# A Mamba kernel whose end-of-chunk states are kept by DMA transfers from ScalarE's queue, where a ScalarE copy kept them

## The reference, cut to what matters

```
xc, z = split(x @ in_w.T);  xc = silu(causal_conv4(xc))
dt, B, C = split(xc @ xp_w.T);  dt = softplus(dt @ dtp_w.T + dtp_b)
h_t = exp(dt_t * A) * h_(t-1) + (dt_t * xc_t) * B_t     # 512 channels x 16 states
y_t = sum over the 16 states of h_t * C_t;  y = (y + xc * D) * silu(z);  out = y @ out_w.T
```

## Time and profile before

| | |
|---|---|
| median of 3 runs | 2550.9 us (2548.64 to 2559.86) |
| the profiled execution | 2551.9 us, span 2550.1 us |
| busy, share of the span | PE 85%, PEld 51%, DVE 74%, ACT 71%, POOL 63% |
| DMA queue that SP issues on | 129732 packets, 181.69 MB, 26.6% of 16 engines |
| `h_carry` copies on ACT | 256, median 193 ns |

### The profile page before, as it was taken

One profiled execution on the slowest core, in us unless ns is written; L12 is line 12 of the kernel. 1 busy time (PEld: TensorE's weight loads), 2 busy tenths in 40 slices (PEclk: granted clock), 3 DMA queues, 4 the chain that ended last, 5 costly groups with the idle time before them and its releaser, 6 DMA issues. The chain is left out here.

```text
span 2550.1 us, 40275 instructions
## 1 busy us (share of the span) xinstructions
PE 2180.0 (85%) x14544; PEld 1305.5 (51%) x14544; DVE 1894.2 (74%) x2586; ACT 1819.4 (71%) x3103; POOL 1615.2 (63%) x1407
## 2 busy tenths in 40 slices
PE   0798898988989989899898998987367699999967
PEld 0345454554545545455454554544234377887744
DVE  4389888898888988889888898888474455555543
ACT  0598889988899888998989989897162244444452
POOL 1089898898988989889898898989310411222010
PEclk9999999999999999999999999999668799999979
DMA  5404224043241532414314143140400211111031
GB/s 188 104 14 117 74 52 117 27 107 77 49 117 35 136 81 53 117 41 93 91 35 117 43 92 92 34 108 17 169 19 29 96 30 34 29 29 29 22 114 66
DMA packets 129930, 184.25 MB, mean 72 GB/s; under 512 B 13634, under 2 KB 76098, under 8 KB 129348
## 3 DMA queue, kind: packets, MB, share of 16 engines
q1 hardware_dynamic: 129732, 181.69, 26.6%
HBM read 134.97 MB, written 42.47 MB: 70 GB/s over the span
## 5 line engine op out<-in xcount | busy, mean ns | idle before, releaser
L617 POOL TENSOR_TENSOR h<-h,C_rep 128x512 f32<-128x512 f32 x1024 | 1274.3, 1277 | 199.4 <-ACT h_carry L536 199.4
L423 DVE TENSOR_TENSOR_SCAN h<-decay,h_carry,psum 128x512 f32<-128x512 f32 x768 | 956.1, 1271 | 126.2 <-PE psum L745 95.3
L528 ACT ACTIVATE decay<-dt_rep,A 128x512 f32<-128x512 f32 x1024 | 729.4, 713 | 101.0 <-DVE h L423 91.8
L745 PEld LDWEIGHTS psum<-ident,u_B 128*128 128x128 f32 x4096 | 476.7, 141 | 561.1 <-DVE h L423 310.2
L745 PE MATMUL psum<-ident,u_B 128*128 128x128 f32 x4096 | 630.4, 280 | 141.2 <-DVE h L423 109.0
L548 ACT ACTIVATE u_B<-u_tok,B_tok 128x512 f32<-128x512 f32 x832 | 589.2, 710 | 63.7 <-PE psum L745 45.9
L423 DVE TENSOR_TENSOR_SCAN h<-decay,zero,psum 128x512 f32<-128x512 f32 x256 | 319.0, 1271 | 54.3 <-PE psum L745 34.6
L754 PE MATMUL psum<-h,state_sum 128*32 128x512 f32 x2048 | 279.7, 619 | 11.1 <-POOL h L617 10.9
L606 POOL TENSOR_TENSOR u_B<-u_tok,B_tok 128x512 f32<-128x512 f32 x192 | 200.1, 1042 | 40.6 <-DVE u_tok L395 40.6
L1590 ACT ACTIVATE a_probs_T<-a_psum 128x512 f32<-128x512 f32 x128 | 76.4, 597 | 197.2 <-PE a_psum L1674 197.2
L1532 DVE TENSOR_REDUCE a_row_max<-a_psum 128x4 f32<-128x512 f32 x128 | 88.4, 691 | 143.3 <-PE a_psum L1665 143.3
(11 more groups left out here) (203 smaller groups left out, 2834.3 us busy)
## 6 DMA issues: line engine op xcount, KB each, us to landing
dt_rep<-dt_rows SPq DMA_DIRECT2D x256, 256.0 KB, 5.6
C_rep<-C_rows SPq DMA_DIRECT2D x256, 64.0 KB, 2.0
dt_rows<-x_dt_gated SPq DMA_DIRECT2D x16, 1024.0 KB, 4.8
x_tok<-mamba_residual SPq DMA_DIRECT2D x16, 512.0 KB
residual<-mamba_residual SPq DMA_DIRECT2D x16, 512.0 KB, 3.9
mamba_residual<-residual SPq DMA_DIRECT2D x16, 512.0 KB, 2.9
f_gru_weights<-in_slot_gru_dram SPq DMA_DIRECT2D x2, 2176.0 KB
n_x<-in_x_dram SPq DMA_DIRECT2D x4, 1024.0 KB, 10.8
```

What stands on the lines that cost most here:

```text
L423: dve.tensor_tensor_scan(h[:, slot(u)], dec[:, u % DEC], PS[:, u % 2], first, ALU.mult, ALU.add)\
L528: act.activation(dec[:, u % DEC], dtr[:, k % EG], ACT.Exp, scale=A[:, s // STEPS, k:k + 1]).then_inc(S["decay"], 1)
L617: pool.tensor_tensor(h[:, slot(u)], h[:, slot(u)], crep[:, k // EG], ALU.mult).then_inc(S["hc"], 1)
L745: ins = pe.transpose(PS[:, u % 2, tb * P:(tb + 1) * P], pr[:, f % 2, tb, eg], ident[:])
```

## The change

The copy in `keep` becomes a DMA that ACT issues, with the same source and destination. It is left out for the last chunk of a sequence (4 of the 16 steps), so 192 transfers take the place of 256 copies. Completion is signalled on four semaphores `h_carry_kept0` to `3` in turn, each raised by 16 by a transfer. POOL waits for the transfer of its quad, or in a last chunk for the four scans themselves. DVE waits for the transfer of the same quad of the chunk before.

```diff
+LANES = 4
+        kept = [sem(f"h_carry_kept{n}") for n in range(LANES)]
+        def last_chunk(q):
+            return q // QUADS % CHUNKS == CHUNKS - 1
+        def carries(q):
+            s = q // QUADS
+            return (s // CHUNKS * (CHUNKS - 1) + s % CHUNKS) * QUADS + q % QUADS
+        def carried(eng, q):
+            eng.wait_ge(kept[carries(q) % LANES], 16 * (carries(q) // LANES + 1))
...
                         if s % CHUNKS:
-                            at(dve, "carry", u // QT - QUADS + 1)
+                            carried(dve, u // QT - QUADS)
...
                 def keep(q):
-                    if not 0 <= q < ALL * QUADS:
+                    if not 0 <= q < ALL * QUADS or last_chunk(q):
                         return
                     at(act, "scan", QT * (q + 1))
                     k = QT * (q % QUADS)
-                    act.activation(carry[:, k:k + QT], h[:, slot(QT * q):slot(QT * q) + QT, T - 1], ACT.Copy)\
-                        .then_inc(S["carry"], 1)
+                    act.dma_start(carry[:, k:k + QT], h[:, slot(QT * q):slot(QT * q) + QT, T - 1], allow_slow_non_contiguous=True)\
+                        .then_inc(kept[carries(q) % LANES], 16)
...
                     if k % QT == 0:
-                        at(pool, "carry", u // QT + 1)
+                        if last_chunk(u // QT):
+                            at(pool, "scan", u + QT)
+                        else:
+                            carried(pool, u // QT)
```

More of the change, by code:

```diff
@@ L246, in mamba @@
                  "x_ev conv_mm conv halo xp_mm dbl silu z_mm z_ev sz dt_mm dt_raw dt bt_mm bt xcT_mm xcT dtT_mm uT skip_mm decay "
-                 "b scan carry hc ysum prod_a prod_p gated o_mm res").split()
+                 "b scan hc ysum prod_a prod_p gated o_mm res").split()
         S = {n: sem(n) for n in names}
         c_ld = [sem(f"C_loaded{n}") for n in range(NG)]
+        kept = [sem(f"h_carry_kept{n}") for n in range(LANES)]
         dtr_ld = [sem(f"dt_rep_loaded{ct}") for ct in range(CT)]
```

## The result

The changed kernel takes 2614.3 us (median of 4 runs, 2607.1 to 2622.8) against 2551.5 us: ratio 1.0242, 95% interval 1.0203 to 1.0281. It is slower, inside the forecast range and 17 us above the forecast number. The time came about as forecast in sign and size, but not where I had put it.

What follows compares the result with a forecast made beforehand. Each step was taken as three stretches in a row, bound by PE, then ACT, then DVE (with POOL). (2.1 + 0.5 + 1.5) x 12 = 49, less 3, on 2551.9 gave 2598 profiled, 2597 us median; range 2553 to 2645.

Steps and rivals of the forecast that it cites:

- ACT's side: ACT's queue: copies removed in its unbroken stretch gain 3 us in all; 192 transfer issues taken to cost nothing, at most 16.
- Term (a): Quad 9, kept at unit 44: POOL begins 2.2 us later for the landing, 2.1 us a step reaching the end.
- the 0.12 us of room: At quad 9: POOL's products ended at 824.98 and `states` began 0.12 us later, so that much lateness is hidden.
- Term (b): Quad 10, kept at 828.69 with the DMA engines busy: landing put at 3.5 us, costing 0.5 us a step.
- Term (c): Keeps while `dt_rep` fills the DMA engines, 842 to 856 us: late landings cost 1.5 us a step, between 0 and 4.0.
- the 3.1 of room: Keep at 843.11, while `dt_rep` comes in: 3.1 us of landing hidden by POOL's later start, `states`' 0.40 and PE's gaps.
- The last chunks: In 4 steps POOL no longer waits for ACT and starts quad 9 sooner: at most 5 us won, taken as nothing.
- B: Rival: no queueing, only the quad 9 landing costs: 2562 to 2573 us, to 2582 with quad 10; chance 0.22.
- C: Rival: full queueing of landings, or a slow issue on ACT besides: 2620 to 2653 us; chance 0.16.
- D: Rival: no measurable change, as a gap takes up the landing or last chunks give their 5 us: 2551; chance 0.11.
- E: Rival: faster, if ACT's slots set the pace everywhere and 26 us go, leaving 2526; chance 0.07.
- The signs I named: Marks of being right: landings 2.5 us, over 4 when full; longer POOL, `states` and DVE waits; steps of 109 and 105 us.

Runs made afterwards that it cites:

- e2: As e1, plus behind each of the 192 copies an ACT-issued transfer of the same shape that no other engine waits for: 2545.1 us, ratio 0.9985.
- e8: Changed kernel, but only quads 12 and 13 of a step (24 of 192) go by transfer, the others by ACT copy: 2622.3 us, ratio 1.0282.
- e10: Changed kernel with SP's dt_rep transfers cut to a quarter of the columns from the second step on: 2555.7 us, ratio 1.0025 against the kernel before.
- e3: Changed kernel, but only quad 9 of each step's 16 quads goes by transfer, the others by ACT copy: 2548.3 us, ratio 0.9991.
- e9: Changed kernel, but quads 12 to 15 go by ACT copy and quads 0 to 11 by transfer: 2551.8 us, ratio 1.0009.
- e6: Changed kernel, but ACT copies three of each quad's four columns and a transfer keeps the fourth; POOL waits for both: 2614.4 us, ratio 1.0245.
- e12: As e8, but PE does 6 and 18 unread transposes ahead of `states` of quads 12 and 13: 2597.0 us, ratio 1.0193 against the kernel before.
- e1: Kernel before with its ACT copies, but nothing kept in the last chunk, where POOL waits for the scans alone: 2546.6 us, ratio 0.9990.
- e7: Kernel before, but POOL copies the four columns itself ahead of its products in chunks 0 to 2, nothing in the last: 2543.9 us, ratio 0.9972.

## Why the prediction came out right, and which of its steps did not

**Sign and cause.** Right: POOL waits for a landing where it waited for a short copy; `states` on PE comes late; nothing behind gives the time back. e2 shows that the issues and packets cost nothing, e8 and e10 that late landings do.

**ACT's side.** Right: an issue is hidden. It is 0.60 us long, not 0.32 to 0.59, and ACT's next `decay` starts beside it. The 3 us gained on ACT can't be told from noise. What I did not draw from it: if the issue runs beside an ACTIVATE, it can also run well ahead of one.

**Term (a), quad 9, 2.1 us a step.** Wrong, and this was the largest term: e3 shows nothing. The landing was near (2.0 us; I took 2.5), and the 0.12 us of room was not put to the test. The step that failed is "POOL begins 2.5 - 0.27 = 2.2 us later where it had been waiting": I let the transfer start where the copy had started. It starts where ACT's queue is, here 2.25 us earlier.

**Term (b), quad 10, 0.5 us.** Wrong in the same way. In step 6 of the changed kernel POOL idles 2.97 us ahead of it, as before (2.99), though the landing took 4.3. The transfer left at 858.49, and the `decay` that stands just behind it in ACT's program began at 862.99: the transfer left 4.50 us before a copy could have begun there. No run had quad 10 alone by transfer, but e9 has it among twelve without loss.

**Term (c), the keeps in the full stretch, 1.5 us a step.** The mechanism was right and the size was too small. e8 puts the whole loss here: 72 us over 12 steps, 6.0 a step; in the changed kernel, 63 over 12, 5.2. I had put 4.1 for a step with all three terms, so the total came near by luck: two errors against each other. The landing was well placed (4.6 taken, 5.1 measured in e8), its reason was not (e6). Two things made it larger. First, I counted quad 13 alone; quad 12 lands late too and PE stalls ahead of both, 1.45 and 1.95 us in step 6. The trace of the kernel before could have told me: its keep of quad 12 stands at 837.47, and SP's first four `dt_rep` had the DMA engines at 0.95 just then:

```profile
834.00:838.00 4.00, 3.45 (x28) 1.96 (x25) 4.00 (x5) 3.67 (x7) 4.00 (x4) 1.00 0.95 221
```

For quad 13 itself the sum holds: it landed after 5.2 us in step 6, which less the 3.1 of room gives 2.1, and PE stood 1.95. DVE's gates behind them wait as well (21.8 us in ten waits). Secondly, I had no term for TensorE's clock: PE stalls at the end of a step, the clock falls, and the next step begins in PE's own stretch at the lower level. e12 gets 25 us of 72 back by filler, two of each step's six. Some of what I call (c) is the first step's too: quad 0's transfer there lands after 11.3 us, and I had no term for the start.

**The last chunks.** The forecast of nothing was right (e1). In the changed kernel steps 3, 7 and 11 are 1.1 to 2.4 us longer than before all the same, though none of their own quads goes by transfer. PE's low clock reaches into them from the end of the step before (it lasts to the first microseconds of step 7), but that this is the cause is not shown: with filler (e12) they take 107.3, 106.5 and 106.7 us, with none (e8) 106.3, 106.5 and 107.4.

**Rivals.** B (only (a), no queueing) had the wrong place. C's full queueing (7.1 us) is not what the median shows. D and E are excluded by the interval; E's argument, 26 us for ACT's slots, is answered by e7, which takes all 256 copies off ACT, puts 192 on POOL and gains 7 us. The signs I named came out mixed. Landings were over 4 us in the full stretch, as named, and 2.0 where I had 2.5. `states` waits for POOL 6.5 us a step ((41.2 + 55.9) / 15), twice the 3 named. Steps of chunks 0 to 2 take 111 us, not 109, and last chunks 108, not 105. POOL's wait at unit 36 was 6.23 us, not over 9, and DVE waits for the transposes behind quad 9 at most 0.8 us (`DVE u_tok L403 <- PE psum L741: 16.4, 28, 0.8`), not near 3: these two are the signs by which (a) fell.

**Open.** What holds a transfer for 2 to 3 us when SP's queue is full, whatever its size; how much of the 47 us is PE's wait itself and how much the gates on DVE; and how the loss divides between quads 12 and 13, as no run had one of them alone.

## What to carry to other kernels

A small DMA in place of an engine's copy cost 2 us of landing here when the DMA engines were quiet, and 4 to 6 when another queue kept them full: before the swap, look at the DMA share at the very moment of each issue, and at who waits for it then. Issued from a queue that is ahead of its engine, the transfer leaves sooner than the copy would have run, which here paid for a quiet landing in full. Price a stall of TensorE together with the clock behind it, above all where the next stretch is TensorE's own.

## What the runs showed of the hardware that I had not expected

- ACT's queue issued a transfer 1.77 us before an ACTIVATE began that stands ahead of it in the program (817.59 against 819.36 in e3).
- An issue takes 0.60 us for 128 x 4 single numbers (192 of them are not seen in the time, e2) and 0.47 for 128 (e6).
- A landing in the full stretch of step 6 takes 4.8 us in the median both with 128 numbers (e6) and with 512 (the changed kernel), against 1.7 and 2.0 in the median of the whole run.
- The transfer issued at 118 us, among the loads of the start, landed after 11.3 us in the changed kernel and after 11.2 in e2, where no other engine waits for it.
- Filler work on TensorE made a kernel 25 us faster, with the mean granted clock going from 0.947 to 0.958.
